# Moving the casts of the middle parts of q and k from VectorE to ScalarE in a fused transformer layer

## The chip, the cores and the metric

The kernel is one program on one core of one Trainium2 chip. The metric is the device time of one execution in microseconds (us). Here the median of three runs stands for the kernel before.

## The reference

The input x has the shape (16, 64, 128, 128): 1024 independent sequences of 128 tokens with 128 features. Each sequence goes through one transformer layer in fp32:

```
q, k, v = x @ wq + bq, x @ wk + bk, x @ wv + bv      (8 heads of 16)
attn    = softmax(q k^T / sqrt(16)) over the 128 keys
x1      = layernorm(x + (attn v) @ wo + bo)
out     = layernorm(x1 + relu(x1 @ w1 + b1) @ w2 + b2)   (hidden width 512)
```

The scores have to be precise to fp32, and the kernel makes them from bf16 products: each of q and k is split into three bf16 parts (high, middle, low) whose sum is the fp32 number.

## The kernel before, in words

The sequences are taken four at a time (`SEQS`), so that a group is 512 tokens and there are 256 groups (`G`). A group goes through a software pipeline over seven steps: in step r the engines work at the same time on q, k and their parts of group r, on the scores of group r-2 (`s_ps`, from which VectorE takes the row maxima), on the transposed scores of groups r-3 and r-4 (`sT_ps`, from which ScalarE makes the exponentials in `prob_sb`), on the attention output of group r-4, and on the feed-forward part and norms of groups r-5 and r-6. Each step has eight units (u = 0 to 7). Every engine runs a list of its own, written out by hand, in the order of the units; an engine never takes a later instruction ahead of an earlier one that waits for its semaphore. The loop is unrolled over 48 steps.

What the change touches is the splitting of q and k (c = 0 is q, c = 1 is k) in step r:

- TensorE multiplies q in unit 2 and k in unit 3 (line 607, into banks B and A).
- ScalarE makes the high part in bf16 (`hi_part`, line 362; q in unit 2, k in unit 3).
- VectorE makes the remainder in fp32 (`rest`, line 451; q in unit 2, k in unit 3).
- VectorE casts the remainder to bf16, the middle part (`mid`, line 459). That of q stands right behind its remainder in unit 2. That of k stands in unit 4, behind `turn_out` (line 466), a 32x32 transpose of the attention output that waits for TensorE.
- GpSimd subtracts the middle part from the remainder, the low part (`lo_part`, line 266, q and then k).
- SyncE waits until both low parts are there and issues twelve DMAs of 128 KB (line 241). They copy the parts into `stack`, where the six products of parts lie below one another as 96 rows, for the scores of step r+2.

SyncE is the only engine that issues DMAs, all on one queue. In step r it issues in this order: three small DMAs of 8 KB that put the negated maxima of group r-3 under the stack (line 221, `stack<-max_parts`), the load of x for group r+1 (line 229), the store of the output of group r-7 (line 232), and the twelve DMAs of group r.

TensorE needs the rows of maxima for the first unit of transposed scores of group r-3, which stands in its unit 4 (line 676). On ScalarE the exponential of a unit (line 379) stands first in its unit. Unit 4 of ScalarE's step is therefore the exponential of unit 0 of group r-3, and then the second relu of the feed-forward part (line 369). `sT_unit` says which unit of which group is due:

```
def sT_unit(u):
    return (4, u + 4) if u < 4 else (3, u - 4)
```

Other lines that the prediction speaks of: 543 to 550 split the maxima (VectorE, unit 0), 684 is the transpose of the maxima on TensorE (unit 0), once a step, and 662 makes the scores.

Of the kernel before, what the change touches and what calls it, by code (L numbers as in the profile page):

```python
# [32 lines left out]
ACT = mybir.ActivationFunctionType  # L33
# [12 lines left out]
HI, MID, LO = range(3)  # L46
# [4 lines left out]
STACK_DMAS = 2 * len(Q_PARTS)  # L51
# [3 lines left out]
DMA = 16  # L55


def build(nc, x, wq, bq, wk, bk, wv, bv, wo, bo, w1, b1, w2, b2, g1, be1, g2, be2, out):
# [7 lines left out]
    with ExitStack() as ctx:  # L66
        def sb(name, shape, dt=F32):
            return ctx.enter_context(nc.sbuf_tensor(name, shape, dt))

        def sem(name):  # L70
            return ctx.enter_context(nc.semaphore(name))
# [19 lines left out]
        parts = sb("parts", [P, 2, 6, T], BF16)  # L91
        rest_sb = sb("rest_sb", [P, 2, T])
# [31 lines left out]
        stack_loaded = [sem("stack_loaded0"), sem("stack_loaded1")]  # L124
# [13 lines left out]
        rest_made, mid_split, max_done, nT_lo, xT_lo = sem("rest_made"), sem("mid_split"), sem("max_done"), sem("nT_lo"), sem("xT_lo")  # L138
# [11 lines left out]
        def live(t, r, lag):  # L150

            return not isinstance(t, int) or 0 <= r - lag < G

        def upto(t, r, lag, per=1, plus=0):


            plus += per * (r - lag)
            if isinstance(t, int):
                return min(plus, per * G) if plus > 0 else None
            return t * per + plus if plus else t * per  # L160

        def upto_dma(t, r, lag, before=0, per=DMA):


            plus = per * ((r - lag) // 2 + 1 - before)
            if isinstance(t, int):
                return plus if plus > 0 else None
            return t * (per // 2) + plus if plus else t * (per // 2)

        def sT_unit(u):  # L170

            return (4, u + 4) if u < 4 else (3, u - 4)

        def iterate(eng, step, begin, first, last, lags):

            for r in range(begin, first):
                step(0, r)
            with eng.Fori(first, last - UNROLL + 1, UNROLL) as t:
                for r in range(UNROLL):
                    step(t, r)  # L180
            for r in range(last, G + lags):
                step(0, r)
# [170 lines left out]
        @block.scalar  # L353
        def _(act):
            act.wait_ge(qk_loaded, N_QK * DMA)

            def hi_part(t, r, c):

                act.wait_ge((q_done, k_done)[c], upto(t, r, 0, plus=1))
                if (v := upto_dma(t, r, 0, before=1, per=STACK_DMAS * DMA)) is not None:  # L360
                    act.wait_ge(stack_loaded[r % 2], v)
                act.activation(parts[:, r % 2, 3 * c + HI], (B, A)[c][:], ACT.Identity,
                               bias=(bq_col, bk_col)[c][:]).then_inc(hi_split, 1)

            def relu(t, r, c):
                act.wait_ge(f1_done, upto(t, r, 5, per=FC, plus=c + 1))
                if (v := upto(t, r, 5, per=2)) is not None:
                    act.wait_ge(f2_done, v)
                act.activation(h_sb[:, c], (C, B)[c % 2][:], ACT.Relu, bias=b1_col[:, c:c + 1]).then_inc(h_ready, 1)  # L369

            def step(t, r):
                for u in range(UNITS):
                    lag, unit = sT_unit(u)
                    if live(t, r, lag):
                        n = (UNITS * (r - lag) + unit)
                        act.wait_ge(sT_done, upto(t, r, lag, per=UNITS, plus=unit + 1))
                        if (v := upto(t, r, lag, per=UNITS, plus=unit - 3)) is not None:
                            act.wait_ge(pv_done, v)
                        act.activation(prob_sb[:, n % 4], sT_ps[n % 2][:], ACT.Exp,  # L379
                                       scale=float(D) ** -0.5).then_inc(exp_done, 1)  # L380
                    if u == 0 and live(t, r, 5):

                        act.wait_ge(shift1_done, upto(t, r, 5, plus=1))
                        if (v := upto(t, r, 5)) is not None:
                            act.wait_ge(nT_done, v)
                        if (v := upto(t, r, 5)) is not None:
                            act.wait_ge(x1g_done, v)
                        for s in range(SEQS):
                            ins = act.activation(n_sb[:, s], z_sb[:, s], ACT.Identity, bias=shift1[:, s:s + 1],  # L389
                                                 scale=rs1[:, s:s + 1])  # L390
                        ins.then_inc(n_done, 1)
                    if u == 7 and live(t, r, 6):

                        act.wait_ge(shift2_done, upto(t, r, 6, plus=1))
                        if (v := upto(t, r, 6)) is not None:
                            act.wait_ge(mg_done, v)
                        for s in range(SEQS):
                            ins = act.activation(m_sb[:, s], y_sb[:, s], ACT.Identity, bias=shift2[:, s:s + 1],  # L398
                                                 scale=rs2[:, s:s + 1])
                        ins.then_inc(m_done, 1)  # L400
                    if u == 1 and live(t, r, 0):
                        act.wait_ge(xT_done, upto(t, r, 0, plus=1))
                        if (v := upto(t, r, 0)) is not None:
                            act.wait_ge(k_done, v)
                        if (v := upto(t, r, 0)) is not None:
                            act.wait_ge(xT_joined, v)
                        act.activation(xT_parts[:, HI], C[:], ACT.Copy).then_inc(xT_hi, 1)
                    if u == 2 and live(t, r, 1):
                        act.wait_ge(v_done, upto(t, r, 1, plus=1))
                        if (v := upto(t, r, 4, per=UNITS)) is not None:  # L410
                            act.wait_ge(pv_done, v)
                        act.activation(v_ones[:, (r - 1) % 4, :, :, 0:D],
                                       A[:].rearrange("p (s h d) -> p s h d", s=SEQS, h=H),
                                       ACT.Copy).then_inc(v_copied, 1)
                    if u == 2 and live(t, r, 5):

                        act.wait_ge(nT_done, upto(t, r, 5, plus=1))
                        if (v := upto(t, r, 5, per=FC)) is not None:
                            act.wait_ge(f1_done, v)
                        act.activation(nT_parts[:, HI], C[:], ACT.Copy).then_inc(nT_hi, 1)  # L420
                    if u == 2 and live(t, r, 0):
                        hi_part(t, r, 0)
                    if u == 3 and live(t, r, 0):
                        hi_part(t, r, 1)
                    if u in (3, 4, 5, 6) and live(t, r, 5):
                        relu(t, r, u - 3)

            step(0, 0)
            act.wait_ge(consts_loaded, N_CONST * DMA)
            act.wait_ge(consts_set, N_SET)  # L430
            step(0, 1)
            act.wait_ge(consts_made, N_MADE)
            iterate(act, step, 2, LEAD, LAST, 6)

        @block.vector
        def _(dve):
# [9 lines left out]
            def rest(t, r, c):  # L446

                dve.wait_ge(hi_split, upto(t, r, 0, per=2, plus=c + 1))
                if (v := upto(t, r, 0, per=2, plus=c - 1)) is not None:
                    dve.wait_ge(lo_split, v)  # L450
                dve.scalar_tensor_tensor(rest_sb[:, c], (B, A)[c][:], (bq_col, bk_col)[c][:],
                                         parts[:, r % 2, 3 * c + HI], ALU.add, ALU.subtract).then_inc(rest_made, 1)

            def mid(t, r, c):

                dve.wait_ge(rest_made, upto(t, r, 0, per=2, plus=c + 1))
                if (v := upto_dma(t, r, 0, before=1, per=STACK_DMAS * DMA)) is not None:
                    dve.wait_ge(stack_loaded[r % 2], v)
                dve.tensor_copy(parts[:, r % 2, 3 * c + MID], rest_sb[:, c]).then_inc(mid_split, 1)  # L459

            def turn_out(t, r, half):

# [41 lines left out]
            def step(t, r):  # L504
                for u in range(UNITS):
                    if u in (0, 4) and live(t, r, 4):
                        turn_out(t, r, u // 4)
                    if u == 4 and live(t, r, 0):
                        mid(t, r, 1)
                    if u in (0, 1) and live(t, r, 6):  # L510
                        add_y(t, r, u)
                    if u == 3 and live(t, r, 0):
# [54 lines left out]
                                          ALU.subtract).then_inc(nT_lo, 1)  # L567
                    if u == 2 and live(t, r, 0):
                        rest(t, r, 0)
                        mid(t, r, 0)  # L570
                    if u == 5 and live(t, r, 6):
                        dve.wait_ge(y_done, upto(t, r, 6, per=2, plus=2))
                        statistics(t, r, 6, y_sb, st2, mv2, st2_done, mv2_done, m_done)

            step(0, 0)
            dve.wait_ge(consts_loaded, N_CONST * DMA)
            dve.wait_ge(consts_set, N_SET)
# [213 lines left out]
```

## Time and profile before

| | |
|---|---|
| median of three runs | 4960.99 us (4960.53 to 4961.19) |
| the profiled execution | 4953.35 us, its span 4951.5 us |
| granted TensorE clock, mean of the span | 0.988 |
| busy: PE, DVE, POOL, ACT | 4482.1, 3946.4, 3634.2, 3387.6 us |
| bytes moved by DMA | 556.46 MB |

The profiled execution is one single execution, and its span runs from the first to the last instruction of the program. Each engine's busy time leaves out waiting, branching and the issuing of DMAs. A row of the profile names the engine, the line, the operation and "out<-in". PE is TensorE's matmuls, PEld its weight loads, DVE VectorE, ACT ScalarE, POOL GpSimd, SPq SyncE's queue of issues.

### The profile page before, as it was taken

What the parts mean: (1) busy time and instruction counts of PE and PEld (TensorE: products, weight loads), DVE (VectorE), ACT (ScalarE), POOL (GpSimd) and SP (SyncE); (2) the same over time, 40 slices, a digit from 0 to 9 for tenths busy, and PEclk for the clock granted to TensorE, in tenths of its full rate; (3) what the DMA queues carried; (4) which work ended last, traced back from release to release, by engine and by line L of the source; (5) the groups of instructions that cost most, each with busy time, mean ns of one, the idle gap of its engine ahead of it and who ended that gap; (6) DMA issues with size and microseconds to landing.
All of it is one profiled execution on the core that took longest, in us unless ns stands there. A gap on an engine that the chain in (4) does not pass through costs nothing.

```text
span 4951.5 us, 159188 instructions
## 1 busy us (share of the span) xinstructions
PE 4482.1 (91%) x51984; PEld 3742.4 (76%) x51984; DVE 3946.4 (80%) x11275; ACT 3387.6 (68%) x6401; POOL 3634.2 (73%) x4620
## 2 busy tenths in 40 slices
PE   4999999989999999899999989999998999999998
PEld 3777777777777777777777777777777777777776
DVE  4888888878888888788888878888887888888886
ACT  2677777667777676677777767777776776777776
POOL 4777777767777777677777767777776777777776
PEclk7999999999999999999999999999999999999999
DMA  8999999989999999899999989999998999999994
GB/s 100 114 115 116 115 114 116 115 108 116 114 115 115 114 115 116 105 116 115 115 114 115 117 106 115 114 115 115 117 113 107 116 115 115 116 114 114 116 116 56
DMA packets 756319, 556.46 MB, mean 112 GB/s; under 512 B 95872, under 2 KB 755328, under 8 KB 755456
## 3 DMA queue, kind: packets, MB, share of 16 engines
q1 hardware_dynamic: 755456, 545.81, 93.1%
q8 instruction: 438, 7.18, 0.8%
q14 instruction: 425, 3.48, 0.4%
HBM read 69.47 MB, written 67.11 MB: 28 GB/s over the span
## 4 chain that ended last, share of the span: by engine, by line
PE 36%; DMA 24%; DVE 21%; issue 8%; SPq 7%; ACT 2%; POOL 1%; DVEq 0%; ACTq 0%; POOLq 0%
DMA stack<-max_parts 24%; PE bankC L629 9%; PE bankA L745 6%; PE oT_ps L645 5%; SPq L221 5%; PE sT_ps L676 4%; DVE st L494 4%; PE s_ps L662 4%; DVE max_sb L535 4%; PE bankB L607 4%; DVE onT_sb L479 3%; PE bankB L629 2%; SPq L241 2%; DVE mv L501 1%; DVE bankA L545 1%
## 5 line engine op out<-in xcount | busy, mean ns | idle before, releaser
L379 ACT ACTIVATE prob_sb<-sT_ps 128x512 f32<-128x512 f32 x2048 | 1221.3, 597 | 1248.5 <-PE sT_ps L676 1248.3
L535 DVE TENSOR_REDUCE max_sb<-s_ps 128x4 f32<-128x512 f32 x2048 | 1380.2, 674 | 153.9 <-PE s_ps L662 151.1
L676 PE MATMUL sT_ps<-stack 99*128 99x128 bf16 x8192 | 800.7, 220 | 224.6 <-DMA stack<-max_parts 223.7
L266 POOL TENSOR_TENSOR parts<-rest_sb,parts 128x512 bf16<-128x512 f32 x512 | 594.9, 1162 | 506.0 <-DVE parts L459 506.0
L662 PE MATMUL s_ps<-stack 96*128 96x128 bf16 x8192 | 813.1, 222 | 44.3 <-issue 31.4
L662 PEld LDWEIGHTS s_ps<-stack 96*128 96x128 bf16 x8192 | 532.6, 98 | 366.6 <-issue 269.1
L676 PEld LDWEIGHTS sT_ps<-stack 99*128 99x128 bf16 x8192 | 539.4, 98 | 267.3 <-DMA stack<-max_parts 265.6
L645 PE MATMUL oT_ps<-prob_sb,v_ones 128*32 128x128 f32 x16384 | 555.1, 276 | 0.0
L466 DVE STREAM_TRANSPOSE ob_sb<-oT_ps 128x512 f32<-128x512 f32 x512 | 364.6, 712 | 219.7 <-PE oT_ps L645 192.8
L629 PE MATMUL bankC<-w_sb,h_sb 128*128 128x128 f32 x4096 | 512.9, 278 | 0.1
L645 PEld LDWEIGHTS oT_ps<-prob_sb,v_ones 128*32 128x32 f32 x16384 | 417.1, 110 | 123.3 <-issue 90.5
L629 PE MATMUL bankB<-w_sb,h_sb 128*128 128x128 f32 x4096 | 503.8, 277 | 0.0
L607 PE MATMUL bankB<-nT_parts,w_parts 128*128 128x512 f32 x1536 | 485.2, 424 | 0.1
L629 PEld LDWEIGHTS bankB<-w_sb,h_sb 128*128 128x128 f32 x4096 | 483.4, 194 | 0.0
L629 PEld LDWEIGHTS bankC<-w_sb,h_sb 128*128 128x128 f32 x4096 | 477.4, 192 | 0.5 <-ACT h_sb L369 0.5
L607 PE MATMUL bankC<-nT_parts,w_parts 128*128 128x512 f32 x1536 | 462.7, 410 | 5.8 <-DVE nT_parts L566 5.8
L327 POOL TENSOR_TENSOR minus_m<-mv,minus_one 128x4 f32<-128x4 f32 x256 | 51.6, 201 | 537.7 <-DVE mv L501 537.7
L398 ACT ACTIVATE m_sb<-y_sb,shift,rs 128x128 f32<-128x128 f32 x1024 | 420.2, 485 | 6.0 <-POOL shift L321 6.0
L745 PEld LDWEIGHTS bankA<-wo_sb,onT_sb 128*128 128x128 f32 x2048 | 249.2, 192 | 229.6 <-issue 216.8
L389 ACT ACTIVATE n_sb<-z_sb,shift,rs 128x128 f32<-128x128 f32 x1024 | 420.4, 485 | 2.2 <-POOL shift L332 2.2
L745 PE MATMUL bankA<-wo_sb,onT_sb 128*128 128x128 f32 x2048 | 295.8, 288 | 121.8 <-DVE onT_sb L479 121.8
L369 ACT ACTIVATE h_sb<-bankB,b_col 128x512 f32<-128x512 f32 x512 | 352.7, 689 | 53.5 <-PE bankB L607 34.0
(80 smaller groups left out, 9260.1 us busy)
## 6 DMA issues: line engine op xcount, KB each, us to landing
stack<-parts SPq DMA_DIRECT2D x3072, 128.0 KB, 6.5
x_sb<-in_x SPq DMA_DIRECT2D x256, 256.0 KB, 5.4
out<-out_sb SPq DMA_DIRECT2D x256, 256.0 KB, 5.4
stack<-max_parts SPq DMA_DIRECT2D x768, 8.0 KB, 6.2
w_sb<-in_L_conv_w SPq DMA_DIRECT2D x2, 256.0 KB, 3.0
be_row<-in_L_conv_ln_b SPq DMA_DIRECT2D x2, 256.0 KB, 19.8
g_row<-in_L_conv_ln_g SPq DMA_DIRECT2D x2, 256.0 KB, 22.8
bo_row<-in_L_conv_bo SPq DMA_DIRECT2D x1, 256.0 KB, 8.7
```

The lines of the kernel that those rows point to most:

```text
L266: pool.tensor_tensor(parts[:, r % 2, 3 * c + LO], rest_sb[:, c], parts[:, r % 2, 3 * c + MID], ALU.subtract).then_inc(lo_split, 1)
L379: act.activation(prob_sb[:, n % 4], sT_ps[n % 2][:], ACT.Exp, scale=float(D) ** -0.5).then_inc(exp_done, 1)
L389: ins = act.activation(n_sb[:, s], z_sb[:, s], ACT.Identity, bias=shift1[:, s:s + 1], scale=rs1[:, s:s + 1])
L398: ins = act.activation(m_sb[:, s], y_sb[:, s], ACT.Identity, bias=shift2[:, s:s + 1], scale=rs2[:, s:s + 1])
L466: dve.transpose(ob_sb[:, half].rearrange("p (s b f d) -> p s f b d", s=2, b=4, f=2), oT_ps[:].rearrange("p (s f b q) -> p s f b q", s=2, f ...
L535: dve.reduce_max(max_sb[:, (r - 2) % 2, half * HU:(half + 1) * HU, s], s_ps[n % 2][:].rearrange("p (h k) -> p h k", h=HU), AX.X).then_inc( ...
L607: ins = pe.matmul(bank, w[:, a], xs[:, b], start=k == 0, stop=k == 2)
L629: ins = pe.matmul((C, B)[half][:, s * P:(s + 1) * P], h_sb[:, c, tok], w2_sb[:, c], start=c == 0, stop=c == FC - 1)
L645: ins = pe.matmul(oT_ps[j * VW:(j + 1) * VW, (unit % 4) * P:(unit % 4 + 1) * P], v_ones[:, (r - lag) % 4, s, h], prob_sb[:, n % 4, j * P:( ...
L662: ins = pe.matmul(s_ps[n % 2][:, j * P:(j + 1) * P], stack[0:PROD, (r - 2) % 4, 0, h, tok], stack[0:PROD, (r - 2) % 4, 1, h, tok], start=T ...
L676: ins = pe.matmul(sT_ps[n % 2][:, j * P:(j + 1) * P], stack[:, (r - lag) % 4, 1, h, tok], stack[:, (r - lag) % 4, 0, h, tok], start=True, ...
L745: ins = pe.matmul(A[:, s * P:(s + 1) * P], onT_sb[:, s * P:(s + 1) * P], wo_sb[:], start=True, stop=True)
```

## The change

Both casts leave VectorE's list and become activations with the function Copy on ScalarE. That of q stands in unit 3 and that of k in unit 4, each behind the exponential of its unit (and in unit 3 behind the high part of k) and ahead of the relu of its unit. The waits for the old contents of `parts` that `mid` had are not repeated, since `hi_part`, earlier on ScalarE, has the same wait.

```diff
+            def mid_part(t, r, c):
+
+                act.wait_ge(rest_made, upto(t, r, 0, per=2, plus=c + 1))
+                act.activation(parts[:, r % 2, 3 * c + MID], rest_sb[:, c], ACT.Copy).then_inc(mid_split, 1)
+
             def relu(t, r, c):
...
                     if u == 3 and live(t, r, 0):
                         hi_part(t, r, 1)
+                    if u in (3, 4) and live(t, r, 0):
+                        mid_part(t, r, u - 3)
                     if u in (3, 4, 5, 6) and live(t, r, 5):
                         relu(t, r, u - 3)
...
-            def mid(t, r, c):
-
-                dve.wait_ge(rest_made, upto(t, r, 0, per=2, plus=c + 1))
-                if (v := upto_dma(t, r, 0, before=1, per=STACK_DMAS * DMA)) is not None:
-                    dve.wait_ge(stack_loaded[r % 2], v)
-                dve.tensor_copy(parts[:, r % 2, 3 * c + MID], rest_sb[:, c]).then_inc(mid_split, 1)
...
                     if u in (0, 4) and live(t, r, 4):
                         turn_out(t, r, u // 4)
-                    if u == 4 and live(t, r, 0):
-                        mid(t, r, 1)
...
                     if u == 2 and live(t, r, 0):
                         rest(t, r, 0)
-                        mid(t, r, 0)
```

## Rows read from the trace of the kernel before

**Rows 1.** The page: busy times; the share of busy DMA engines in 40 slices; the queue

```profile
PE 4482.1 (91%) x51984; PEld 3742.4 (76%) x51984; DVE 3946.4 (80%) x11275; ACT 3387.6 (68%) x6401; POOL 3634.2 (73%) x4620
...
DMA  8999999989999999899999989999998999999994
...
q1 hardware_dynamic: 755456, 545.81, 93.1%
```

**Rows 2.** The page's chain of work that ended last, by line

```profile
DMA stack<-max_parts 24%; PE bankC L629 9%; PE bankA L745 6%; PE oT_ps L645 5%; SPq L221 5%; PE sT_ps L676 4%; DVE st L494 4%; PE s_ps L662 4%; DVE max_sb L535 4%; PE bankB L607 4%; DVE onT_sb L479 3%; PE bankB L629 2%; SPq L241 2%; DVE mv L501 1%; DVE bankA L545 1%
```

**Rows 3.** The waits, whole span: who for whom, us in total, times, longest

```profile
ACT prob_sb L379 <- PE sT_ps L676: 1248.3, 1028, 9.8
...
PE sT_ps L676 <- DMA stack<-max_parts: 223.7, 231, 7.7
...
PE s_ps L662 <- issue: 31.4, 4, 8.0
```

**Rows 4.** The waits of SyncE's queue, same columns

```profile
SPq L241 <- POOL parts L266: 1380.6, 255, 8.3
```

**Rows 5.** Line 684 on TensorE, once a step: ns min/median/max, first and last start

```profile
L684 PE MATMUL bankA<-ident,max_sb x256: 274/274/421, 70.0 to 4900.0; 128*32 128x128 f32 x128
```

**Rows 6.** Timeline of SyncE's queue, 2559 to 2606 us: start, length, queue, line

```profile
2566.94 7.79 SPq L241 DMA_DIRECT2D stack<-parts  x12
2577.20 1.82 SPq L221 DMA_DIRECT2D stack<-max_parts  x3
...
2586.05 9.13 SPq L241 DMA_DIRECT2D stack<-parts  x12
...
2604.63 1.91 SPq L241 DMA_DIRECT2D stack<-parts  x3
```

**Rows 7.** Chain in order of time, 2559 to 2605 us: start, length, what

```profile
2559.96 5.84 DMA stack<-max_parts
...
2578.43 5.90 DMA stack<-max_parts
...
2596.95 6.49 DMA stack<-max_parts
```

**Rows 8.** Timeline, 2559 to 2588 us, around the splitting of one group

```profile
2577.29 0.60 ACT L379 ACTIVATE prob_sb<-sT_ps 128x512 f32<-128x512 f32 x1 [0.21 <-PE sT_ps L676]
...
2577.78 0.59 ACT L407 ACTIVATE xT_parts<-bankC 128x512 fp32r<-128x512 f32 x1
...
2580.55 0.69 ACT L362 ACTIVATE parts<-bankB,bq_col 128x512 bf16<-128x512 f32 x1
...
2582.49 0.75 DVE L451 SCALAR_TENSOR_TENSOR rest_sb<-bankA,bk_col,parts 128x512 f32<-128x512 f32 x1
...
2583.75 0.71 DVE L466 STREAM_TRANSPOSE ob_sb<-oT_ps 128x512 f32<-128x512 f32 x1
...
2584.37 0.40 PE L676 MATMUL sT_ps<-stack 99*128 99x128 bf16 x4 [0.61 <-DMA stack<-max_parts]
2584.38 0.39 DVE L459 CAST parts<-rest_sb 128x512 bf16<-128x512 f32 x1
...
2584.80 0.60 ACT L379 ACTIVATE prob_sb<-sT_ps 128x512 f32<-128x512 f32 x1 [1.58 <-PE sT_ps L676]
2584.85 1.17 POOL L266 TENSOR_TENSOR parts<-rest_sb,parts 128x512 bf16<-128x512 f32 x1 [1.13 <-DVE parts L459]
```

**Rows 9.** Groups of instructions, whole span: busy us, mean ns, idle before

```profile
L459 DVE CAST parts<-rest_sb 128x512 bf16<-128x512 f32 x512 | 208.9, 408 | 19.4
...
L362 ACT ACTIVATE parts<-bankB,bq_col 128x512 bf16<-128x512 f32 x256 | 176.3, 688 | 38.8 <-PE bankB L607 25.9
...
L412 ACT ACTIVATE v_ones<-bankA 128x512 f32<-128x512 f32 x256 | 153.1, 598 | 71.8 <-PE bankA L703 71.8
```

**Rows 10.** Two stretches: busy PE, PEld, DVE, ACT, POOL, then PE clock, DMA share, GB/s

```profile
2529.00:2533.00 4.00, 4.00 (x24) 3.09 (x22) 3.02 (x12) 2.49 (x5) 2.97 (x6) 0.57 0.79 119
...
2566.00:2568.00 2.00, 2.00 (x18) 1.42 (x16) 1.15 (x4) 1.56 (x3) 2.00 (x3) 1.00 0.02 6
```

## The prediction

> **What bounds the kernel now.** I read the page first. No engine is full: PE is busy for 91% of the span, DVE for 80%, ACT for 68%, and the DMA queue's packets fill 93.1% of the sixteen engines' time [rows 1]. With four parties that near to one another the shares decide nothing, so I went on to the chain of work that ended last. Its largest entry by far is a transfer, the three small DMAs of maxima, with 24% of the span [rows 2]. They carry only 24 KB a step, so their length is not their own size but what lies ahead of them. The waits say who suffers: PE waits for these rows in 231 of the 256 steps, and ACT's exponentials wait for PE for 1248.3 us [rows 3]. SyncE's queue waits for the low parts once in each step, 1380.6 us in all, 5.4 us a step [rows 4]. So the twelve large DMAs are issued late and not for want of a free issuer.
>
> Now the order in time. The rows of maxima land at the end of each of three pieces of the chain: 2565.80, 2584.33 and 2603.44 us [rows 7]. The first of the twelve DMAs is issued at 2566.94, 2586.05 and 2604.63 us [rows 6]. From the first issue of one step to the landing in the next is therefore 17.4 us, both times. The maxima are issued at 2577.20 us, 7.1 us before they land: they stand in the same rings behind 1.5 MB of parts. After the landing the DMA engines are empty: from 2566 to 2568 us their share is 0.02 [rows 10], until the new parts begin to flow.
>
> From a landing to the first issue of the step behind it takes 20.25 us (2565.80 to 2586.05) and 20.30 us (2584.33 to 2604.63). This way leads through PE's list to the high part of q at 2580.55, the remainder of k, the transpose of the attention output, the cast at 2584.38, the low part at 2584.85 and the issue at 2586.05 [rows 6, 8]. Both together are a loop that closes over two steps: 17.4 + 20.3 = 37.7 us, or 18.85 us a step. The trace as a whole has 255 intervals of line 684 between 70.0 and 4900.0 us, 18.94 us each [rows 5]; four stalls of PE of some 8 us at the ends of the unrolled body [rows 3], 31.4 us or 0.12 a step, bring that to 18.8. I take **18.8 us a step now**, so that the mean distance from first issue to landing is 2 x 18.8 - 20.3 = **17.3 us**.
>
> What matters for the change: in each step the landing comes near the cast of k (2584.33 and 2584.38), but the cast doesn't depend on it. It depends on the landing of the step before.
>
> **The change, part by part.**
>
> (1) VectorE loses 512 casts of 408 ns, 208.9 us busy [rows 9]. The one of k stood on the loop, 0.39 us behind the transpose of 0.71 us [rows 8]. Taken alone this would be a gain: the remainder of k is done at 2583.24, the cast started at 2584.38, so its input lay idle for 1.14 us.
>
> (2) ScalarE gains 512 copies. The trace has no copy from SBUF to bf16. The nearest rows are a copy of the same size from PSUM, 598 ns, and, as upper end, an activation with a bias column and bf16 output, 688 ns [rows 9]. I take 0.60, since the new one has no bias. ACT gets 0.3 ms more busy time, 74% of a span like this one: it does not become full.
> The Trainium skill ("VectorE: DVE Perf Modes", section on the TRN2 errata) gives ScalarE a larger fixed cost from SBUF than from PSUM, 224 against 172 cycles at 1.2 GHz; by that the copy would be an estimated 0.04 us longer, and the total some 10 us more. No row here shows this pair.
>
> (3) The cast of q goes from behind its remainder to unit 3, behind the high part of k. It may end some 0.4 us later. I cost it at nothing: its low part is the first of two on POOL, which then sits idle for 1.13 us before the second [rows 8]. Without that cover it would cost its 0.4 us.
>
> (4) The cast of k now stands behind the exponential of unit 4 on an engine that keeps its order. That exponential needs the scores for which PE waits until the rows of maxima land. This is a new wait. The issue of the twelve DMAs thus hangs on the landing of the **same** step. From the landing: scores and start of the exponential 0.47 (2584.33 to 2584.80); the next activation starts 0.49 behind the start of an exponential (2577.29, 2577.78); the copy 0.60; to the start of the low part 0.08 (cast's end 2584.77 to 2584.85); the low part 1.17; to the issue 0.03 [rows 8, 6]. The sum is 2.84 us. Now it is 1.14, 1.72 and 1.19 us in the three steps.
> The loop closes over one step: 2.84 + 17.3 = **20.1 us a step**. The bounds are the copy at 0.69 and the distance at the 17.4 of the rows, or longer by as much again, 17.6, for 20.5; and the distance at 17.0, if the emptier rings help by 0.3, with the spacing 0.1 shorter, for 19.7.
>
> (5) Is the old way still covered? The input of the copy of k is ready 17.4 us behind the previous landing (2565.80 to 2583.24), and the copy would start at 20.1 + 0.96 = 21.1. So the way through PE has 3.6 us to spare. What is queued behind the new copies on ACT, the second relu and the later exponentials, moves by a few tenths. PE, normalisation and the statistics wait for those, all inside the 3.6 us. That PE's arrival gets earlier against the landing buys nothing. The maxima reach the rings about 11 us behind a landing (2577.20 against 2565.80), long ahead of the 20.1 at which they would land, so their own issue isn't on the loop either. The order on SyncE stays; its queue waits longer for the low parts.
>
> (6) Steps with both a splitting and a wait for maxima are 3 to 255, 253 of them. 253 x (20.1 - 18.8) = 329 us. The ramps at both ends and the stalls I leave as they are. The profiled execution of 4953.35 us (span 4951.5) becomes 5282 us. The median of the runs stands 7.6 us above it, so the forecast is 4961 + 329 = **5290 us**.
>
> **The rivals.**
>
> *A weaker loop.* DMA engines that rest longer move the parts faster, and the twelve DMAs land sooner. For it: the queue is busy for 93.1% and its share would fall. Against it: the two distances in the rows are equal, 17.4, though the idle times ahead of them were 1.14 and 1.72 us. At 19.7 us a step it gives 253 x 0.9 = 228 us, 5189 us. Chance 0.09.
>
> *The clock of TensorE.* PE would stand idle for some 2.2 us in every step, where the wait now has 223.7 / 231 = 1.0 [rows 3]. In this trace the granted clock fell to the lower of its levels (1.2 against 2.4 GHz) right after one such wait: 2529 to 2533 us has a mean of 0.57 [rows 10]. That fall cost at most (1 - 0.57) x 4 = 1.7 us, less than the 3.6 us to spare, so falls of that length add nothing. It decides where more is lost: PE has 4482.1 / 256 = 17.5 us of work a step [rows 1], and if the clock were low for a third of it, 5.8 us of work would take twice as long, 2.2 us over the cover: 253 x (1.3 + 2.2) = 886 us, 5847 us. Chance 0.05 for a visible addition.
> The Trainium skill ("TensorE: Matmul & The Clock Gate", Part 1) has an idle array throttled to half its rate until it has been busy again; by that rule falls become more frequent here, which the row of one fall bears out, and whether they get past the cover it does not say.
>
> *Faster.* The rows of maxima land before ACT reaches unit 4, so that the exponential holds nothing up. Then the copy of k follows its remainder at once: the issue comes 0.60 + 0.08 + 1.17 + 0.03 = 1.88 us behind 2583.24, at 2585.12 instead of 2586.05, 0.93 us a loop of two steps: 253 x 0.46 = 118 us less, 4843 us. It decides where the distance from first issue to landing is below about 14 us (17.4 - 0.96 - 2.84 = 13.6). Nothing in the rows is near that. Chance 0.03.
>
> *No effect.* The diff does what it says, and I see no way in which ScalarE could take the copy of k earlier; what is left is that losses and gains cancel. Chance 0.02.
>
> **How the numbers follow.** The forecast has 0.81 with bounds from 19.7 to 20.5 us a step, 5189 to 5391 us. The range I give is 5205 to 5375. What a measurement here can tell from no change is about 0.2%, 10 us. Faster 0.03, same 0.02, slower 0.95.
>
> **What the profile after would show.** First issues of line 241 some 20.1 us apart and evenly, not 18.5 and 19.1 by turns; 2.8 us from the landing of the maxima to that issue; the copy of k right behind the exponential of unit 4, and POOL's low part waiting for ACT. PE's wait for the maxima near 2.2 us a step, 550 us in all; the DMA queue at about 87%; SyncE's wait for the low parts above 1900 us. The forecast is wrong if the distance from first issue to landing isn't 17 to 17.6 us, or if the copy of k starts ahead of the exponential.

## The result and the profile after

The kernel after takes 5296.74 us in the median of four runs (5292.37 to 5299.93). The kernel before took 4960.76 us beside it. The ratio is 1.0677, with a 95% interval of 1.0658 to 1.0695. The forecast was 5290 us, within 5205 to 5375. The profiled execution took 5296.75 us, its span is 5294.5 us.

The page of the kernel after, the lines that answer to [rows 1]:

```profile
PE 4620.8 (87%) x51984; PEld 3862.5 (73%) x51984; DVE 3789.0 (72%) x10763; ACT 3593.1 (68%) x6913; POOL 3618.5 (68%) x4620
...
DMA  7989898989899998899898988998988998989894
...
q1 hardware_dynamic: 755456, 545.81, 87.4%
```

Every engine's share is lower or the same. ScalarE has 512 more activations and still 68% of the span, as before. An engine that got full isn't what happened.

The waits of the kernel after, which answer to [rows 3, 4]; the last line is of SyncE's queue, the others are of the engines:

```profile
POOL parts L266 <- ACT parts L368: 1090.4, 509, 12.6
...
PE sT_ps L673 <- DMA stack<-max_parts: 448.9, 245, 8.5
```

```profile
SPq L241 <- POOL parts L266: 1892.5, 255, 13.8
```

PE's wait for the rows of maxima has doubled, from 223.7 us. SyncE's wait for the low parts has grown by 512 us. POOL now waits for ScalarE's copy, line 368.

The timeline of the kernel after in the same stretch, which answers to [rows 8]: start, length, engine, line.

```profile
2561.20 0.40 PE L673 MATMUL sT_ps<-stack 99*128 99x128 bf16 x4 [1.21 <-DMA stack<-max_parts]
...
2564.02 8.36 SPq L241 DMA_DIRECT2D stack<-parts  x12
...
2578.04 0.75 DVE L458 SCALAR_TENSOR_TENSOR rest_sb<-bankA,bk_col,parts 128x512 f32<-128x512 f32 x1 [0.39 <-ACT parts L362]
...
2581.38 0.40 PE L673 MATMUL sT_ps<-stack 99*128 99x128 bf16 x4 [2.07 <-DMA stack<-max_parts]
...
2581.81 0.60 ACT L384 ACTIVATE prob_sb<-sT_ps 128x512 f32<-128x512 f32 x1 [2.70 <-PE sT_ps L673]
2582.30 0.62 ACT L368 ACTIVATE parts<-rest_sb 128x512 bf16<-128x512 f32 x1
...
2583.00 1.16 POOL L266 TENSOR_TENSOR parts<-rest_sb,parts 128x512 bf16<-128x512 f32 x1 [3.17 <-ACT parts L368]
...
2584.19 1.25 SPq L241 DMA_DIRECT2D stack<-parts  x2
```

Read from the bottom, this is the loop. The twelve DMAs of this step are issued from 2584.19 on, right behind the low part of k (the window ends behind the second of them). That waited 3.17 us for the copy, the copy stood behind the exponential, the exponential waited for PE, and PE for the rows of maxima. Those were held in the rings by the twelve DMAs that were issued at 2564.02. The remainder of k, the copy's only real input, was ready at 2578.79; it lay there for 3.51 us. From one first issue to the next it takes 20.17 us.

The other steps agree. In the steps 10 to 249 of both traces the median distance from the first issue to the landing of the maxima is 17.29 us, before and after. What changed is the way from the landing to the next first issue: 1.48 us before, 2.87 us after.

The transpose of the maxima, once a step, gives the mean (it answers to [rows 5]):

```profile
L681 PE MATMUL bankA<-ident,max_sb x256: 274/274/421, 71.7 to 5243.0; 128*32 128x128 f32 x128
```

(5243.0 - 71.7) / 255 = 20.28 us, against 18.94: 1.34 us more, 255 times, gives 342 of the 343 us between the two spans.

One view misleads. In the chain of work that ended last the kernel after shows less of the transfer than before, not more ([rows 2] had 24%):

```profile
DMA stack<-max_parts 12%; SPq L241 8%; PE bankB L604 5%; PE bankC L626 4%; PE bankA L742 4%; PE sT_ps L673 4%; PE s_ps L659 3%; PE bankB L626 3%; PE oT_ps L642 2%; POOL o_sb L274 2%; PE bankC L604 2%; SPq L221 2%; POOL mg_sb L338 2%; POOL x1g_sb L293 2%; POOL parts L266 2%
```

The chain follows a transfer back to its own issue, and from there through the engines. What stands ahead of it in the rings it can't see, and that is where this loop goes. The pairs of issue and landing in the timeline show it.

### The profile page after: what moved, and what is told of

Its sections match the earlier page's. It is cut to its first block, busy times and chain, and to the rows that moved or that the text cites. A ratio compares the mean times of both kernels' runs of the same rounds, so it can differ in the third digit from the quotient of the medians.

```text
span 5294.5 us, 159160 instructions
## 1 busy us (share of the span) xinstructions
PE 4620.8 (87%) x51984; PEld 3862.5 (73%) x51984; DVE 3789.0 (72%) x10763; ACT 3593.1 (68%) x6913; POOL 3618.5 (68%) x4620
## 3 DMA queue, kind: packets, MB, share of 16 engines
q1 hardware_dynamic: 755456, 545.81, 87.4%
q14 instruction: 417, 3.42, 0.4%
## 4 chain that ended last, share of the span: by engine, by line
PE 29%; issue 26%; DMA 13%; POOL 11%; SPq 10%; DVE 7%; ACT 3%; POOLq 0%; ACTq 0%; DVEq 0%
DMA stack<-max_parts 12%; SPq L241 8%; PE bankB L604 5%; PE bankC L626 4%; PE bankA L742 4%; PE sT_ps L673 4%; PE s_ps L659 3%; PE bankB L626 3%; PE oT_ps L642 2%; POOL o_sb L274 2%; PE bankC L604 2%; SPq L221 2%; POOL mg_sb L338 2%; POOL x1g_sb L293 2%; POOL parts L266 2%
## 5 line engine op out<-in xcount | busy, mean ns | idle before, releaser
L673 PE MATMUL sT_ps<-stack 99*128 99x128 bf16 x8192 | 836.6, 226 | 449.0 <-DMA stack<-max_parts 448.9
L673 PEld LDWEIGHTS sT_ps<-stack 99*128 99x128 bf16 x8192 | 567.2, 101 | 493.0 <-DMA stack<-max_parts 491.4
L659 PE MATMUL s_ps<-stack 96*128 96x128 bf16 x8192 | 845.0, 228 | 34.6 <-issue 23.9
L659 PEld LDWEIGHTS s_ps<-stack 96*128 96x128 bf16 x8192 | 553.5, 102 | 386.9 <-issue 318.3
L604 PE MATMUL bankB<-nT_parts,w_parts 128*128 128x512 f32 x1536 | 537.1, 462 | 0.1
L604 PE MATMUL bankC<-nT_parts,w_parts 128*128 128x512 f32 x1536 | 513.0, 446 | 5.8 <-DVE nT_parts L564 5.8
L374 ACT ACTIVATE h_sb<-bankC,b_col 128x512 f32<-128x512 f32 x512 | 352.7, 689 | 63.7 <-PE bankC L604 63.6
```

The costliest lines, as they stand in the source:

```text
L604: ins = pe.matmul(bank, w[:, a], xs[:, b], start=k == 0, stop=k == 2)
L659: ins = pe.matmul(s_ps[n % 2][:, j * P:(j + 1) * P], stack[0:PROD, (r - 2) % 4, 0, h, tok], stack[0:PROD, (r - 2) % 4, 1, h, tok], start=T ...
L673: ins = pe.matmul(sT_ps[n % 2][:, j * P:(j + 1) * P], stack[:, (r - lag) % 4, 1, h, tok], stack[:, (r - lag) % 4, 0, h, tok], start=True, ...
```

## The experiments

The theory of the loop: landing of the maxima, exponential of unit 4, copy of k, low part, first issue, and through the rings to the next landing. Its rivals: the load (ScalarE has more to do, so all behind it is late), and the clock. Besides those: is the distance from issue to landing really volume, and not latency?

Steps are the mean from line 684 (or its like) over 255 intervals. Each ratio is to the kernel before as it ran beside that kernel, 4956.7 to 4960.8 us in the median.

| kernel | median us | ratio to before, 95% | step us |
|---|---|---|---|
| after | 5296.7 | 1.0677 (1.0658 to 1.0695) | 20.28 |
| only the cast of k moved | 5296.2 | 1.0681 (1.0663 to 1.0698) | 20.28 |
| only the cast of q moved | 4946.5 | 0.9978 (0.9968 to 0.9987) | 18.90 |
| one more activation, unit 4 | 5418.8 | 1.0923 (1.0904 to 1.0941) | 20.78 |
| one more activation, unit 6 | 5294.6 | 1.0674 (1.0656 to 1.0691) | 20.27 |
| PE kept busy ahead of its wait | 5298.6 | 1.0684 (1.0666 to 1.0701) | 20.29 |
| copy of k ahead of the exponential | 4871.9 | 0.9822 (0.9805 to 0.9838) | 18.62 |
| the same, q on VectorE | 4857.0 | 0.9793 (0.9777 to 0.9809) | 18.55 |
| before, k's cast at once | 4917.4 | 0.9914 (0.9897 to 0.9930) | 18.79 |
| after, a thirteenth DMA | 5622.5 | 1.1345 (1.1326 to 1.1364) | 21.53 |
| after, maxima on ScalarE's queue | 5377.2 | 1.0853 (1.0835 to 1.0871) | 20.56 |
| the same, k ahead, q on VectorE | 5007.3 | 1.0099 (1.0083 to 1.0116) | 19.21 |
| DMAs of parts as they are made | 4698.1 | 0.9477 (0.9461 to 0.9493) | 17.94 |

**Which of the two casts.** Each is moved alone; where the two engines share a counter, the cast of k also waits for that of q. This is the edit for k; for q it has u == 3, and the cast that isn't moved stands in VectorE's list at its old place.

```diff
-                    if u in (3, 4) and live(t, r, 0):
+                    if u == 4 and live(t, r, 0):
                         mid_part(t, r, u - 3)
```

Only k:

> The kernel after, but the cast of q is VectorE's again, behind its remainder in unit 2; only the cast of k is ScalarE's, behind the exponential of unit 4. The loop theory (landing of the maxima, exponential of unit 4, copy of k, low part, issue, landing): all of the slowdown is there, 5290 to 5300 us, 2.87 us from landing to first issue. The load theory (ScalarE has 0.3 ms more to do and everything behind it is late): half of the slowdown, some 5130 us.

Only q:

> The kernel after, but the cast of k is VectorE's again in unit 4, at its old place (with a wait for the cast of q, so that the two count in order); only the cast of q is ScalarE's, in unit 3. The loop theory: as before the change, 4961 us within 10, since the low part of k still starts last. The load theory: half of the slowdown, some 5130 us.

All of the slowdown comes with the cast of k, 5296.2 us, and none with that of q. That halves don't each bring a half speaks against the load. The cast of q alone is even 0.22% faster, where no change was expected. Of the 8.8 us between the two spans 6 are in the four stalls at the ends of the unrolled body: PE waited for issue 25.4 us there, as this row of its waits shows, where [rows 3] have 31.4. Why, isn't known.

```profile
PE s_ps L670 <- issue: 25.4, 4, 7.0
```

**The same work in two places.** One activation a step that nobody needs, first on the loop, in unit 4, and in a second kernel off it, in unit 6.

```diff
+                    if u == 4 and live(t, r, 0) and live(t, r, 3):
+                        act.activation(extra[:], w1g_sb[:], ACT.Copy)
                     if u in (3, 4) and live(t, r, 0):
                         mid_part(t, r, u - 3)
...
+                    if u == 6 and live(t, r, 0) and live(t, r, 3):
+                        act.activation(extra[:], w1g_sb[:], ACT.Copy)
```

In unit 4:

> The kernel after with one more activation a step on ScalarE, a copy of 128x512 fp32 from SBUF into a tile that nobody reads, between the exponential of unit 4 and the copy of k. The loop theory: the step grows by the spacing of two such activations, 0.5 us, 253 times, so 5297 + 130 = 5425 us, and landing to first issue goes from 2.87 to 3.4 us. The load theory: slower too, by as much as the next kernel of this call. The clock theory (PE's falls to 1.2 GHz make the slowdown): only as far as the clock falls more.

In unit 6:

> The same additional activation, but in unit 6 behind the relu, where ScalarE waits for PE. The loop theory: nothing, 5297 us within 10. The load theory: the same as with the activation in unit 4, about 5425 us.

The timeline of the kernel with the activation in unit 4:

```profile
2562.02 0.48 PE L676 MATMUL sT_ps<-stack 99*128 99x128 bf16 x4 [2.21 <-DMA stack<-max_parts]
...
2562.54 0.60 ACT L385 ACTIVATE prob_sb<-sT_ps 128x512 f32<-128x512 f32 x1 [2.94 <-PE sT_ps L676]
...
2563.04 0.62 ACT L432 ACTIVATE extra<-w1g_sb 128x512 f32<-128x512 f32 x1
...
2563.56 0.62 ACT L369 ACTIVATE parts<-rest_sb 128x512 bf16<-128x512 f32 x1
...
2565.44 9.48 SPq L242 DMA_DIRECT2D stack<-parts  x12
```

From PE's start to the first issue it is now 3.42 us instead of 2.82. The spacing of the activations, 0.52 us, goes into the step almost whole (20.28 to 20.78) and costs 122 us. Off the loop 253 more activations of the same length cost nothing. Load isn't the cause; place is.

**The clock.** The kernel after has a mean granted clock of 0.958 where before had 0.988, and PE's busy time rose by 139 us with the same matmuls. Keeping PE at work ahead of its wait takes that away:

```diff
-                        for j in range(HU):
+                        for j in [j for _ in range(8 if u == 4 else 1) for j in range(HU)]:
                             h = HU * (u % 2) + j
                             ins = pe.matmul(s_ps[n % 2][:, j * P:(j + 1) * P], stack[0:PROD, (r - 2) % 4, 0, h, tok],
```

> The kernel after, but TensorE makes the four score products of unit 4 eight times over (same operands, same bank, same result), some 1.6 us of additional work a step just ahead of its wait for the maxima. The loop theory: PE only waits less, the landing isn't earlier, the time stays at 5297 us within 15, whatever the granted clock does. The clock theory (the falls to 1.2 GHz, 97 of them behind the ramp against 10 before, carry part of the slowdown): the clock rises towards 0.98 and the time falls by tens of us or more.

The clock rose to 0.99, PE's wait for the maxima fell, and the time stayed:

```profile
PE sT_ps L673 <- DMA stack<-max_parts: 129.9, 236, 6.4
```

So the lower clock was a consequence of the waits, and the cover held it. In the steps 10 to 249 of the kernel after the remainder of k lay ready for 3.4 us in the median and for 1.3 us at the least; with PE kept busy the least is 2.8 us. The falls of the clock used up part of the cover of 3.6 us, but never all of it.

**Is it volume?** A thirteenth DMA of the same size stands ahead of the twelve.

```diff
-STACK_DMAS = 2 * len(Q_PARTS)
+STACK_DMAS = 2 * len(Q_PARTS) + 1
...
                     sp.wait_ge(lo_split, upto(t, r, 0, per=2, plus=2))
+                    sp.dma_start(spare[:, r % 2], parts[:, r % 2, HI]).then_inc(stack_loaded[r % 2], DMA)
```

> The kernel after with a thirteenth DMA of 128 KB in each step, ahead of the twelve, from the same parts into a tile nobody reads. The loop theory holds the distance from first issue to landing of the maxima for the volume that stands ahead of them in the rings: twelve take 16.6 us, of which 1.5 pass before the first bytes, so one more is 1.26 us a step, 253 times, 5297 + 319 = 5615 us, and the distance goes from 17.3 to 18.6. A theory in which the distance is a latency, or is set by SyncE's issuing (8.6 of the 17.3 us): no change, 5300 us.

Timeline of this kernel:

```profile
2571.30 0.61 SPq L240 DMA_DIRECT2D spare<-parts  x1
...
2590.03 0.40 PE L675 MATMUL sT_ps<-stack 99*128 99x128 bf16 x4 [1.56 <-DMA stack<-max_parts]
...
2592.84 0.60 SPq L240 DMA_DIRECT2D spare<-parts  x1
```

From the first issue to PE's start it takes 18.73 us, against 17.36 in the kernel after (2564.02 to 2581.38); the step grew by 1.26 us, the time by 326. The distance grows with the volume ahead of the maxima, as told, and a plain latency is ruled out. SyncE's issuing doesn't set the distance either: in this kernel the last of the parts is issued at 2579.74, and the maxima follow at 2581.92 and land only 8 us later.

**A queue of their own.** On another queue the maxima shouldn't have to wait for the parts. The first lines are of SyncE's list, the second of ScalarE's:

```diff
-                    sp.wait_ge(max_parts_made, upto(t, r, 3, plus=1))
-                    for part in range(MAXROWS):
-                        sp.dma_start(stack[PROD + part:PROD + part + 1, (r - 3) % 4, 0],
-                                     max_parts[:, part]).then_inc(max_rows_loaded, DMA)
...
+                    if u == 1 and live(t, r, 3):
+                        act.wait_ge(max_parts_made, upto(t, r, 3, plus=1))
+                        for part in range(MAXROWS):
+                            act.dma_start(stack[PROD + part:PROD + part + 1, (r - 3) % 4, 0],
+                                          max_parts[:, part]).then_inc(max_rows_loaded, DMA)
```

> The kernel after, but the three small DMAs of maxima are issued by ScalarE, on its own queue, at the end of its unit 1 (behind the high part of x); the other DMAs stay on SyncE's queue. If the maxima are late because they stand behind the parts in one queue, they now land some 16 us or less behind the landing before, the loop through the copy of k is open, and what PE and the other engines need for a step remains, 18.2 to 18.6: 4800 to 4900 us. If the sixteen engines serve both queues in the order of issue, or ScalarE loses by issuing what it wins, near 5300 us.

> The same, with the copy of k ahead of the exponential of unit 4 and the cast of q on VectorE. If the queue is what made the maxima late, the place of the copy hardly matters any more: within 1% of the kernel above, and no slower than 4857 us. If the queue makes no difference: 4857 us plus what the issuing costs ScalarE.

Both missed. Timeline of the first, issues on ScalarE's queue (ACTq) and PE's wait:

```profile
2574.94 7.72 SPq L236 DMA_DIRECT2D stack<-parts  x12
...
2584.22 0.51 ACTq L411 DMA_DIRECT2D stack<-max_parts  x1
...
2584.76 1.25 ACTq L411 DMA_DIRECT2D stack<-max_parts  x2
```

```profile
2592.39 0.40 PE L673 MATMUL sT_ps<-stack 99*128 99x128 bf16 x4 [1.46 <-DMA stack<-max_parts]
```

From the first issue of the parts to PE's start it is 17.45 us, about as on the shared queue. The maxima, the last of them issued 6.4 us before, still count as landed only when the parts are through. Another queue doesn't overtake.

It even costs time, in two ways. In both kernels the mean distance from the first issue to the landing is longer, in the first 17.67 us against 17.33 on the shared queue (steps 10 to 249), which alone covers its 0.28 us a step; why it is longer, no run shows. And ScalarE loses the time of issuing, three times 0.5 to 0.6 us ahead of its next exponential. The first kernel's cover hides that. The second has no such cover: its way from a landing to the next high part of q is 15.6 us where it was 14.8, and it loses 150 us (5007.3 against 4857.0). The Trainium skill ("DMA: Bandwidth & Descriptors", section on queues, rings and completion order) says that a DMA's semaphore is written only after every earlier write of the same DMA engine, across its queues, and that both queues run on the same sixteen engines. These rows agree with it.

**The place of the copy of k.** It goes ahead of the exponential, which is what follows `sT_unit`:

```diff
+                    if u == 4 and live(t, r, 0):
+                        mid_part(t, r, 1)
                     lag, unit = sT_unit(u)
                     if live(t, r, lag):
...
-                    if u in (3, 4) and live(t, r, 0):
+                    if u == 3 and live(t, r, 0):
                         mid_part(t, r, u - 3)
```

> The kernel after, but in unit 4 the copy of k stands ahead of the exponential, and so no longer behind the landing. Both casts stay on ScalarE. The loop theory: the loop closes over two steps again, and k's low part starts as soon as q's is done on POOL; first issue 4.9 us behind the start of q's high part where it was 5.5 before the change, 0.3 us a step less than before: 4880 us (bounds 4840 to 4960). The load theory (two more activations a step on ScalarE are what costs): near 5290 us.

With the cast of q on VectorE again:

> As the one above, with the cast of q VectorE's again. The loop theory: q's low part is done earlier on POOL and k's waits only for its copy: 4.65 us from the start of q's high part to the first issue, 0.43 us a step less than before the change: 4850 us. If the two-step loop isn't what bounds any more, the gain stops short of that.

Two lines exchanged on ScalarE make 425 us, and turn the loss into a gain against both kernels. Timeline of the first:

```profile
2575.30 0.63 ACT L368 ACTIVATE parts<-rest_sb 128x512 bf16<-128x512 f32 x1
...
2576.88 0.40 PE L675 MATMUL sT_ps<-stack 99*128 99x128 bf16 x4 [1.27 <-DMA stack<-max_parts]
2577.20 3.20 SPq L241 DMA_DIRECT2D stack<-parts  x5
```

The copy ends ahead of the landing, and the first issue no longer depends on the landing of its own step. (The row of issues ends with the window; there are twelve, as ever.) Here the two low parts follow each other on POOL without a pause, so that the cast of q, moved too, is what is late: with q on VectorE it is 4857.0 us, and the idea was to be had with half of the change.

**The same gain without ScalarE.** The kernel before, with VectorE's cast of k moved forward:

```diff
                     if u == 3 and live(t, r, 0):
                         rest(t, r, 1)
+                        mid(t, r, 1)
...
-                    if u == 4 and live(t, r, 0):
-                        mid(t, r, 1)
```

> The kernel before, nothing moved to ScalarE: the cast of k stands on VectorE right behind its remainder in unit 3 and no longer behind the transpose of unit 4. The loop theory: the first issue comes 1.1 us earlier, 0.55 us a step, 4820 us. A theory in which VectorE's order of maxima and transposes bounds the loop: no gain or a loss, since both come 0.4 us later.

It gains 0.9% and not 2.8%. The groups of instructions of this kernel show a part of the reason, to be read beside [rows 9], where the same 512 casts took 408 ns:

```profile
L459 DVE CAST parts<-rest_sb 128x512 bf16<-128x512 f32 x512 | 316.2, 618 | 28.1
```

The timeline has the other part: the cast of k now runs while POOL makes the low part of q.

```profile
2561.19 1.17 POOL L266 TENSOR_TENSOR parts<-rest_sb,parts 128x512 bf16<-128x512 f32 x1 [0.65 <-DVE parts L459]
2561.90 0.73 DVE L459 CAST parts<-rest_sb 128x512 bf16<-128x512 f32 x1
2562.55 0.68 DVE L534 TENSOR_REDUCE max_sb<-s_ps 128x4 f32<-128x512 f32 x1
...
2563.16 0.70 DVE L466 STREAM_TRANSPOSE ob_sb<-oT_ps 128x512 f32<-128x512 f32 x1
```

It takes 0.73 us instead of 0.39, and everything behind it on VectorE moves back by the whole of it. The first issue does come earlier, 4.7 us behind the start of q's high part where it was 5.5, but the way from a landing to the next high part of q gets 0.4 us longer (medians of the steps 10 to 249). ScalarE's copy, 0.63 us, had no such effect, so here ScalarE is the better engine for k, if it stands in the right place. That the two engines hinder each other was not tried alone. The traces speak for it: in this one the 255 casts that overlap the subtraction take 0.69 to 0.91 us and those that overlap no work of GpSimd 0.43 us, and in the kernel before only 3 of the 512 casts overlap it; they take up to 0.82 us, and all others 0.43 at the most.

**The version that beats both.** If the first issue is what closes the loop, it needn't wait for the low parts at all. Ten of the twelve DMAs carry high and middle parts. On the base of the 4857.0 us kernel:

```diff
-                    sp.wait_ge(lo_split, upto(t, r, 0, per=2, plus=2))
-                    for j in range(len(Q_PARTS)):
-                        for c, part in enumerate((Q_PARTS[j], K_PARTS[j])):
+                    for due, made in ((HI, hi_split), (MID, mid_split), (LO, lo_split)):
+                        sp.wait_ge(made, upto(t, r, 0, per=2, plus=2))
+                        for j in range(len(Q_PARTS)):
+                            for c, part in enumerate((Q_PARTS[j], K_PARTS[j])):
+                                if part == due:
```

> The kernel with the copy of k ahead of the exponential and the cast of q on VectorE (4857 us), and SyncE no longer waits for both low parts before it issues anything: it issues the six DMAs of high parts once k's high part is made, the four of middle parts once k's is made, and the two of low parts last. The loop theory: the first issue comes some 2.5 to 3 us earlier, the loop over two steps loses that, and the step falls until the next bound: PE's list and the DMA engines' own traffic, both 17.6 to 18.0 us: 4720 to 4780 us. If what matters is when the low parts are issued (the last of the twelve), the gain is small: above 4830 us.

4698.1 us, 5.2% under the kernel before. PE waits for the maxima twice in the whole span and no longer in every step, and the queue is busy for 83.6% of it:

```profile
PE sT_ps L684 <- DMA stack<-max_parts: 10.4, 2, 9.7
```

```profile
q1 hardware_dynamic: 755456, 545.81, 83.6%
```

The first issue stands 1.9 us behind the start of q's high part, where it was 4.7 in the kernel that this one builds on. The loop through the rings no longer sets the step, with the same bytes. What bounds now is most likely PE, 4435.2 us busy in a span of 4696.1; that is read from its share and was not tried. The measured time lies 22 us below the expected 4720 to 4780 us.

## Why the prediction was right

- *The loop over two steps before.* Right. Earlier first issues shorten the step, by 0.32 and 0.39 us in the two kernels with the copy of k ahead, where 0.3 and 0.43 were expected.
- *The copy of k behind the exponential closes the loop over one step* (step 4 of the working). Right, in every term. Landing to first issue was given as 2.84 us; the rows show 2.81 and 2.82 from PE's start, which comes 0.05 behind the landing, so 2.86 to 2.87. The distance through the rings stayed at 17.3. The step was given as 20.1; the first issues stand 20.17 us apart.
- *The copy's length* was taken as 0.60 us, from a copy out of PSUM. It is 0.622, as the row below shows. The Trainium skill's pair of fixed costs for SBUF and PSUM ("VectorE: DVE Perf Modes", section on the TRN2 errata) would have added an estimated 0.04; the rows show 0.024 more than the copy out of PSUM in [rows 9]. ScalarE's busy time was to rise by 0.3 ms and rose by 206 us, since neighbouring activations overlap: they start 0.5 us apart and last 0.6. Nothing in the forecast hung on it.

```profile
L368 ACT ACTIVATE parts<-rest_sb 128x512 bf16<-128x512 f32 x512 | 318.5, 622 | 0.8 <-DVE rest_sb L458 0.6
```

- *The cast of q costs nothing.* Right for the kernel after: with q on VectorE it takes the same. Moved alone it even gave 11 us. It had a price only once k's copy was in the right place: 15 us, between 4871.9 and 4857.0.
- *The way through PE is covered by 3.6 us.* Right: the copy's input lay ready for 3.51 us. The clock fell more often, as the rival had it, and added nothing, as the forecast had it. What the 550 us of the forecast left out is that PE's work gets longer when the clock falls: its wait for the maxima is 448.9 us, not 550, with 139 us more of busy time beside it.
- *The rival of a weaker loop* fell: the parts moved no faster for a longer rest, 17.29 us in the median before and after.
- *The rival of a gain* fell for the reason given: ACT reaches unit 4 ahead of the landing. Its mechanism is sound. Exchanging the two lines puts it to work, and brought 1.8% against its 2.4%, since POOL's two low parts then stand one behind the other.
- *The signs to look for.* Evenly spaced issues: the next first issue after those shown is at 2604.29, 20.10 us on, so 20.17 and 20.10 where it was 19.11 and 18.58. The DMA queue at 87.4%: as told. SyncE's wait for the low parts was to be above 1900 us and is 1892.5.
- *The remaining 7 us.* The step grew by 1.34 us and not by 1.3. Both steps were rounded to 0.1 us, and half of that is 13 us of time, so a miss of 7 us is in part luck.

## What to carry to other kernels

Before an instruction is moved to an engine that has time to spare, look at what stands ahead of it there and what that waits for: on an engine that keeps its order it inherits the wait, here 3.5 us for a copy whose input was ready. Where a result goes out by DMA and a small transfer follows on the same engines, the issue and the small one's landing are a loop, and the chain of work doesn't show it; write down issue and landing side by side. And issue each transfer as soon as its own data is made.

## What the runs showed of the hardware

- Three small DMAs, issued by another engine on another queue behind 1.5 MB of transfers, landed no earlier than on the same queue: 17.45 us from the parts' first issue to the start of the matmuls that wait for them, against 17.36. Each of the three issues took ScalarE 0.5 to 0.6 us.
- The distance from issue to landing didn't depend on how long the DMA engines had rested: its median was 17.29 us both where the first issue came 1.48 us behind the last landing and where it came 2.87 us behind it. One more DMA of 128 KB added 1.26 us to the step.
- A cast on VectorE from SBUF to bf16, 128x512, took 0.39 to 0.43 us alone and 0.69 to 0.91 us while GpSimd ran a subtraction on SBUF; the same conversion on ScalarE took 0.62 to 0.63 us, alone or beside the subtraction. The Trainium skill ("GPSIMD Engine Reference", section 1) names SBUF interfaces that the two engines share; no run here separates that from other causes.
- TensorE's mean granted clock went from 0.988 to 0.958 with waits of about 2 us in each step, and to 0.99 when these were filled with work, without any effect on the time.
